# A four-layer transformer kernel on one core: score masks leave TensorE, spreading of keys and values moves to GpSimd and VectorE, feed-forward in half-pairs, new orders

## The reference

```python
# layer 0: adapter with one of 16 experts per sequence
h = gelu(x @ down_W.T + down_b)                        # 128 -> 32
h = h @ expert_W[id0].T + expert_b[id0] + domain_emb[id0]
x = layernorm(h @ up_W.T + up_b + x) * ln_gamma + ln_beta
# layer 1: attention with a bias and a key mask per sequence, 16 heads of 8
scale, shift = split(silu(sin_emb(timestep)) @ W_ada + b_ada)
x = layernorm(x) * (1 + scale) + shift
s = (x @ Wq + bq) / sqrt(8) @ (x @ Wk + bk).T + attention_bias
s = where(src_mask, -inf, s)
x = x + softmax(s) @ (x @ Wv + bv) @ Wo + bo
h = layernorm(x) * g2 + beta2
x = x + gelu2(h @ W1 + b1) @ W2 + b2                   # 128 -> 512 -> 128, gelu2(y) = y * sigmoid(1.702 y)
# layer 2: feed-forward with one of 8 experts per sequence
x = layernorm(gelu(x @ Wi[id2] + bi[id2]) @ Wo[id2] + bo[id2] + x) * gamma[id2] + beta[id2]
# layer 3: causal attention and feed-forward, gated
h = layernorm(x) * gamma1 + beta1
s = where(causal, (h @ Wq + bq) @ (h @ Wk + bk).T / sqrt(8), -inf)
x1 = x + softmax(s) @ (h @ Wv + bv) @ Wo + bo
h2 = layernorm(x1) * gamma2 + beta2
x2 = x1 + gelu(h2 @ W1 + b1) @ W2 + b2
out = x + g * (x2 - x)
```

## Time and profile before

| what | us |
|---|---|
| median of 3 runs | 180.58 |
| lowest, highest run | 177.86, 183.02 |
| span of the profiled execution | 176.3 |
| TensorE, VectorE, ScalarE, GpSimd busy | 138.0, 118.7, 93.9, 15.5 |

### The profile page before, as it was taken

One profiled execution on the slowest core, in us unless ns is written; L12 is line 12 of the kernel. 1 busy time (PEld: TensorE's weight loads), 2 busy tenths in 40 slices (PEclk: granted clock), 3 DMA queues, 4 the chain that ended last, 5 costly groups with the idle time before them and its releaser, 6 DMA issues.

```text
span 176.3 us, 6271 instructions
## 1 busy us (share of the span) xinstructions
PE 138.0 (78%) x2582; PEld 101.3 (57%) x2582; DVE 118.7 (67%) x340; ACT 93.9 (53%) x188; POOL 15.5 (9%) x22
## 2 busy tenths in 40 slices
...
GB/s 73 203 222 283 390 376 233 197 204 210 212 213 204 201 4 0 4 2 18 237 224 219 170 206 209 194 224 227 7 2 4 35 4 4 0 33 0 0 0 59
DMA packets 10970, 23.39 MB, mean 133 GB/s; under 512 B 2302, under 2 KB 5286, under 8 KB 10943
## 3 DMA queue, kind: packets, MB, share of 16 engines
...
...
...
## 4 chain that ended last, share of the span: by engine, by line
PE 51%; DVE 21%; issue 7%; ACT 7%; SPq 5%; DMA 4%; POOL 3%; DVEq 0%; POOLq 0%
PE ps L534 9%; PE ps L542 8%; PE ps L561 5%; DMA kex<-in_rows 4%; PE ps L550 4%; PE ps L390 3%; PE ps L485 3%; DVE nrm L687 3%; DVE bn L770 3%; DVE res L691 3%; PE ps L480 2%; PE ps L508 2%; PE ps L470 2%; PE ps L529 2%; PE ps L475 2%
## 5 line engine op out<-in xcount | busy, mean ns | idle before, releaser
L534 PE MATMUL ps<-xt,tab 128*128 128x256 f32 x64 | 18.4, 439 | 1.6 <-DVE xt L787 1.3
L620 ACT ACTIVATE lnv<-mv,eps 128x2 f32<-128x2 f32 x24 | 7.0, 293 | 22.6 <-DVE mv L773 22.3
L542 PE MATMUL ps<-tab,pt 128*128 128x128 f32 x128 | 16.8, 281 | 0.0
L534 PEld LDWEIGHTS ps<-xt,tab 128*128 128x128 f32 x64 | 13.7, 225 | 4.2 <-issue 2.2
L542 PEld LDWEIGHTS ps<-tab,pt 128*128 128x128 f32 x128 | 15.6, 192 | 0.2
L803 DVE SCALAR_TENSOR_TENSOR kex<-ps,bqk,tab 128x512 f32<-128x512 f32 x16 | 11.9, 745 | 3.3 <-PE ps L485 3.3
L649 ACT ACTIVATE pt<-ps,tab 128x256 f32<-128x256 f32 x32 | 12.5, 477 | 1.5 <-PE ps L534 1.3
L593 ACT ACT_TABLE_LOAD x9 | 11.5, 1283 | 2.7 <-DVE mv L773 2.0
L470 PE MATMUL ps<-tab,res 128*128 128x128 f32 x16 | 3.7, 320 | 11.7 <-DVE res L691 11.7
L639 ACT ACTIVATE pt<-ps 128x512 f32<-128x512 f32 x16 | 9.4, 594 | 4.2 <-PE ps L508 4.1
L631 ACT ACTIVATE qt<-ps,bqs 128x128 f32<-128x128 f32 x16 | 5.8, 364 | 10.1 <-PE ps L475 10.1
...
## 6 DMA issues: line engine op xcount, KB each, us to landing
...
```

Source lines behind the costliest of these rows:

```text
L534: mm = pe.matmul(ps[:, BANK_OF[name, i] + c // 2, (c % 2) * 2 * P:(c % 2 + 1) * 2 * P], col("w1" + layer, c * P, P), tok, start=True, stop ...
L542: mm = pe.matmul(y, hg[:, i, c, n * P:(n + 1) * P], col("w2" + layer, c * D, D), start=False, stop=(c == C - 1))
```

## The change

- **Masks.** The mask matmuls go. In layer 1 a new step `fm` adds the mask to the fside tile in SBUF (seven on GpSimd, `fm.3` on VectorE); in layer 3 a new step `sb3` on VectorE adds the causal table while it moves the scores from PSUM to SBUF, and `mx3`, `sub3` work in SBUF.
- **Projections.** `qk1`/`qk3` make queries and keys of a pair of tiles, with 256 columns a matmul; `v1`/`v3` keep their small matmuls. ScalarE evicts queries, keys and values (`qe`, `ke`, `ve`). `kx` and `vx` then spread from SBUF to SBUF: 11 `kx` and 10 `vx` stand on GpSimd, 5 `kx` and 6 `vx` on VectorE. Six of the 16 `sub` stand on GpSimd too.
- **Feed-forward** runs in half-pairs: `ff`, `act` and `fo` take two of the four 128-wide chunks at a time, in one bank.
- **Evictions** are divided anew: eight `evpt`, four `evct`, one `eve1`, one `ev_d` go to VectorE, seven of the twelve `ev_c`, `ev_f`, `ev_g` to ScalarE.
- **Head.** The adaptive rows use one float32 table (`emb`, `oh3f`) in place of three bfloat16 terms, so `w_embc` has two operations instead of five. `xub` and `res0` work on pairs, the loads are cut and ordered anew, `w_oh2` moves to GpSimd. The warm-up has 9 matmuls of 512 columns instead of 36 of 128.
- **Zero products.** Eight `fill` steps multiply zeros, 19 matmuls of 512 columns in all.
- **Waits.** A counter now belongs to a kind of step and an engine; waits that an earlier wait of the engine covers, and those in `KNOWN`, are not issued.
- **Orders** of all five engines are new.

```diff
-WARM_UP = 36
+WARM_UP = 9
...
+FILL = {0: 2, 1: 5, 2: 3, 3: 1, 4: 2, 5: 4, 6: 1, 7: 1}
+KNOWN = """
+expert.0:w_selc down.1:ebias ada.1:res0 expert.1:gelu0 up.1:gelu0 up.1:ebias up.1:w_embc up.1:w_selc w_bi.0:res0
...
-BANKS = {"w_sel": 2, "w_bi": 2, "up": 4, "sc1": 4, "ff1": 2, "sc3": 4, "ff3": 2}
+BANKS = {"w_sel": 2, "w_bi": 2, "up": 4, "sc1": 4, "sc3": 4}
...
+        def ready(eng, name, tiles, first=None):
+
+            for engine, count in value_of(name, tiles, tiles - 1 if first is None else first).items():
+                signal = kind_of(name), engine
+                if waited.get((eng, signal), 0) < count:
+                    waited[eng, signal] = count
+                    eng.wait_ge(done[signal], count)
...
+                if name == "fill":
+                    for _ in range(FILL[i]):
+                        pe.matmul(dst, idle_bf[:, 0:P], idle_bf[:], start=True, stop=True)
+                    continue
...
+                    tok = xt[:, ts[0]:ts[-1] + 1, :].rearrange("p t s -> p (t s)")
+                    for n in range(2):
+                        mm = pe.matmul(dst[:, n * 2 * P:(n + 1) * 2 * P], col("wqkv" + layer, n * D, D), tok,
+                                       start=True, stop=True)
...
-                    for g in range(HG):
-                        pe.matmul(ps[:, at + g, 0:P].rearrange("p (h s) -> p h s", h=H4), ident_bf[:],
-                                  masked[:, None, :].broadcast_to([P, H4, S]), start=True, stop=False)
...
+                    u, half = i // 2, i % 2
+                    ready(pe, "ev_c" if layer == "1" else "ev_g", 2 * u + 2)
+                    tok = xt[:, 2 * u:2 * u + 2, :].rearrange("p t s -> p (t s)")
+                    for n in range(2):
+                        mm = pe.matmul(dst[:, n * 2 * P:(n + 1) * 2 * P], col("w1" + layer, (2 * half + n) * P, P), tok,
+                                       start=True, stop=True)
...
+                elif name in ("ke1", "ke3"):
+                    ready(act, "qk" + layer, t1)
+                    act.wait_ge(loaded["bqk"], 32)
+                    n = 0 if layer == "1" else 1
+                    ins = act.activation(kt[:, t0:t1, :].rearrange("p t s -> p (t s)"), bank("qk" + layer, i)[:, 2 * P:4 * P],
+                                         ACT.Identity, bias=bqk[:, n, 1:2])
...
+                elif name == "sb3":
+                    ready(dve, "sc3", t1)
...
+                    ins = dve.tensor_tensor(sc[:, i].rearrange("p (g h) s -> p g h s", g=HG), scores("sc3", i),
+                                            col("causal")[:, None, None, :].broadcast_to([P, HG, H4, S]), ALU.add)
...
+                elif name == "fm":
+
+                    ready(pool, "w_neg", 1)
+                    pool.wait_ge(fs_landed[i], 16)
+                    ins = pool.tensor_tensor(sc[:, i], sc[:, i], mask_neg[:, i, None, :].broadcast_to([P, H, S]), ALU.add)
+                elif name in ("kx1", "kx3"):
+
+                    ready(pool, "ke" + layer, i + 1)
...
+                    ins = pool.tensor_tensor(kex[:, i], kt[:, i, None, :].broadcast_to([P, H4, P]),
+                                             col("head_mask")[:, :, None].broadcast_to([P, H4, P]), ALU.mult)
...
 POOL_ORDER = """
-w_adb.0 w_oh3.0 xub.0 w_pre.0 w_rows.0 w_neg.0 xub.1 w_bis.0
+xub.0 w_oh2.0 xub.1 w_oh3f.0 w_bqs.0 w_pre.0 w_neg.0 fm.1 xub.3 w_oh3.0 xub.2 w_rows.0 fm.0 fm.5 fm.4 kx1.1
+kx1.3 kx1.2 fm.2 vx1.1 vx1.0 kx1.7 vx1.3 vx1.2 fm.6 fm.7 kx1.5 kx1.6 vx1.7 w_bis.0 vx1.5 sub1.6 kx3.0 kx3.1
```

More of the change, by code:

```diff
@@ L72 @@
 GRAIN = {
-    "w_oh0": 1, "w_ang": 1, "w_oh2": 1, "w_pre": 1, "w_adb": 1, "xub": 4, "w_oh3": 1, "w_neg": 1, "w_rows":
-    1, "w_silu": 1, "w_sel": 1, "w_selb": 1, "w_selc": 1, "w_sbc": 1, "w_emb": 1, "w_embc": 1, "w_bi": 1,
-    "w_bic": 1, "w_bis": 1, "fs": 1, "down": 4, "gelu0": 4, "expert": 4, "ebias": 4, "up": 4, "res0": 4,
-    "stat_a": 2, "rstd_a": 2, "aff_a": 2, "stat_b": 2, "rstd_b": 2, "ada": 2, "aff_b": 2, "tr_b": 2, "ev_b":
-    2, "q1": 1, "qe1": 1, "kv1": 1, "kex1": 1, "vbd1": 1, "sc1": 1, "sb1": 1, "mx1": 1, "sub1": 1, "exp1":
```

496 lines of the change are left out of this document (291 added, 205 removed), and 5 rows, old and new, of the table GRAIN.

## The result

The changed kernel takes 169.03 us (median of 4 runs, 164.66 to 171.62) where the kernel before took 180.12 beside it: a ratio of 0.926, 95% interval 0.913 to 0.940. Six later runs gave 167.52 us and 0.928 (0.920 to 0.936). The medians are those of all runs; a ratio and its interval leave out runs over 1.5% above the fastest of their kernel, and where too few are left no ratio is given. The profiled execution took 166.91 us, its span is 165.1.

What follows compares the result with a forecast made beforehand. The prediction saw a chain-bound head, TensorE and VectorE taking turns, then TensorE bounding. Its terms: 24 + 30 + 9 + 2 = 65 us to the mark, 93 behind, 2.9 end, 4.3 outside the span: 165 us, range 150 to 178.

Steps and rivals of the forecast that it cites:

- The head: Stretch up to layer 1's first transpose, `tr_b.0`: forecast at 24 us instead of 34.16, winning 10 us, bounds 7 and 12.
- VectorE's 30 us: VectorE's own work from `aff_b.0` at about 24 us up to `mx1.6`: 17.4 + 5.0 + 7.8 us.
- GpSimd's hold: Before the mark, 19 VectorE operations with two SBUF inputs wait for GpSimd: 9 us, bounds 0 and 19.
- the mark: End of `pt1.6`, last but one transpose of layer 1's probabilities: 84.4 us before, forecast at 65 us, bounds 59 and 75.
- the first half: From `tr_b.0` to the mark; a clock fall there, with too few zero products to prevent it, would prove the forecast wrong.
- The part behind the mark: From the mark to the last matmul: 80 us of TensorE work plus 13 us idle (bounds 5 and 20), 93 us.
- TensorE's savings: TensorE work saved: 5.3 us by dropping mask matmuls, 3.2 us by making q and k for pairs of tiles.
- Weights: Behind the mark, expert weight loads do not bind: 16 loads took 37.6 us, against some 44 us of TensorE work.
- Outside the span: Old median 180.58 us less old profiled span 176.3: 4.3 us, added unchanged to the forecast span of 161 us.
- TensorE bounded: Rival: TensorE bounds all of the kernel, the orders hiding GpSimd and evictions; 150 us, chance 0.2.
- The norms do wait: Rival: `norm_c`, `norm_f`, `norm_g` are held up by GpSimd like two-input operations; 4 us more, 169 us, chance 0.1.
- GpSimd's hold throughout: Rival: 30 two-input VectorE operations each wait for a whole GpSimd operation, and GpSimd for them; about 200 us, chance 0.06.

Runs made afterwards that it cites:

- second profile: The changed kernel run again unaltered, six runs with another profiled execution: median 167.52 us, ratio 0.928.
- the four edits: Changed kernel without zero products, with `ada` in bfloat16, `fm.1` behind `aff_a` on GpSimd and `w_bi` moved behind `qk1.0`: 161.76 us, ratio 0.900.
- neither burst of zero products: Zero products added ahead of `tr_b.0`: eight in the changed kernel with `w_bi` moved behind `qk1.0`, 168.72 us; five in the kernel with the four edits, 162.30 us.
- the burst ahead of `tr_b.0`: Changed kernel with eight zero products right ahead of `tr_b.0`, where `w_bi` stood, and `w_bi` moved behind `qk1.0`: 168.72 us.
- the bfloat16 kernel: Changed kernel with the `ada` tables (`emb`, `oh3f`) in bfloat16 instead of float32, losing precision: 164.86 us, ratio 0.917.

## Why the prediction came out right

The time is 169.03 us where 165 was forecast, within its range, and the sign is right. Its sum was 65 + 93 + 2.9 + 4.3; the profiled execution has 73.2 + 88.9 + 3.0 + 1.8 = 166.9. Two errors of 8 and 4 us went against each other, and one term meant something else: that the time came out within 4 us is in part luck.

**The head**, 24 us forecast, came at 27.07, just outside its 22 to 27. The term that failed is TensorE's, not GpSimd's: the float32 `ada` was put at 0.8 us, from no row, and the zero products of the head at next to nothing, at the clock of 2.4 GHz, though the earlier trace rows shows transposes at the slower pace (0.66 us for two). At 1.2 GHz `ada.0` and `ada.1` took 3.78 us, two `fill` 3.77, and `w_bi`, which I did not count at all, 3.19. Taking most of this away, together with GpSimd's hold on `aff_a`, brought `tr_b.0` to 22.06 us and the end with it. GpSimd did cost `aff_a` 3.9 us, more than the bound of 3, but in the changed kernel this lay beside TensorE's queue; with `ada` alone shortened it came to the fore (32.26 us).

**VectorE's 30 us** up to `mx1.6` were right. From the end of `aff_b.0` (25.8 us) to the end of `mx1.6` (70.1) VectorE is busy for 34.6 us. Of this some 4 are waits inside operations (`norm_c` 1.0, `fm` and `kx` 0.9 each, `sub1` 0.7, `aff` 0.5), which leaves about 30.6 us of its own. **GpSimd's hold** was 4 us, not 9 (second profile: some 6; with the four edits 10.7): GpSimd was busy for 25.45 of the 46.1 us from `tr_b.0` to the mark, a good half, where I had put three quarters. **The step that failed** is what I left out: VectorE's waits. It had work for 30 us and 9.7 us of idle time among it, mostly for TensorE: 3.1 for `ada.2`, 1.9 for scores, 1.5 for `wo1.0`, 1.5 for keys by way of ScalarE. So 25.8 + 30.6 + 4.0 + 9.7 and 3.1 for `sub1.6`, `exp1.6` and the transposes make the 73.2. I had said that I would be wrong if TensorE's clock fell in the first half. It was at 1.2 GHz for 37.6 us, and yet neither burst of zero products that raised it earlier made the kernel faster, nor was the changed kernel's second profile shorter in this stretch, where the clock rose 9 us earlier by itself. The kernel before had run its head at 1.2 GHz too. Two engines that take turns bound this stretch, and when the head was shortened (22.06 us) VectorE filled it, for a quarter of it held up by GpSimd. How many of the 9.7 us are the clock's and how many the order's is not settled; that the burst ahead of `tr_b.0` took 44.5 us is within what single executions differ by.

**The part behind the mark**, 80 of work and 13 of idle, measured 79.35 and 9.55. That its work is the same on both sides was right; the allowance for new waits was too high.

**TensorE's savings**, 5.3 us of masks and 3.2 of pairings, were counted as work, and as time they hardly exist: the masks put back cost 1.2 us in the median, within its uncertainty (in the profiles 2 us at most behind the mark, nothing ahead of it), the pairing nothing that shows, since 128 columns cost half of 256. **The skipped waits** of `KNOWN` cost nothing that shows, as forecast. **Weights**: no wait of TensorE for a transfer, as forecast. **GpSimd's operations**, forecast at 1.26 us: `kx` 1.31, `vx` 1.14, `sub` 1.06, `fm` 1.39. That GpSimd's operations are not longer beside VectorE's, as I read the earlier trace rows, did not hold (last section). `sub1` and `sub3` on VectorE took 0.79 us on average, over the 0.68 that was the sign.

**Outside the span**: 4.3 us was the median of some executions less the span of another. Those of the changed kernel took 1.8 us more than their own span, those of the kernel before 1.8 to 3.0.

**The rivals.** TensorE bounded 18 us of the first half, at 1.2 GHz, and not all of it. The norms do wait: `norm_c` took 1.59 us for its pair beside GpSimd's `w_bis`, and the 16 operations of `norm_c` and `norm_f` 450 ns on average where they took 341 before, which is 1.7 us in all, ahead of the mark; none behind it waited. This agrees with the Trainium skill, "GPSIMD Engine Reference", Specifications, where operations in the 2-port mode contend with GpSimd beside those with two SBUF inputs; which of VectorE's operations are in that mode no row shows, only that these wait. GpSimd's hold throughout (200 us) is far off: twice the spreads cost 9.3 us.

Where, then, did 11.2 us of span come from? 7.1 from the head, 4.6 from the stretch up to the mark, -0.5 from the rest. For the head the kernels with the four edits show that a shorter one reaches the end in full (5.85 us of head, 7.3 of span); a longer one need not, as in the bfloat16 kernel, 4.35 us later at `tr_b.0` than the second profile and 0.5 at the end. For the 4.6 us I can show only what it isn't: not masks, pairing, zero products or skipped waits. VectorE is busy for less there (36.3 us, some 4.6 of it held up, where it was 38.6 in the stretch of the earlier trace rows), since GpSimd took part of its work; whether that or the order made the 4.6 was not tried apart.
